# Softmax attention on one core: the row maxima turned in float16 into the sums' bank, the scores 64 times smaller, and the output product moved beside the value block

## The reference, cut to what matters

```python
q = split_heads(x @ Wq.T)
k = split_heads(x @ Wk.T)
v = split_heads(x @ Wv.T)
sim = jnp.einsum('bhid,bhjd->bhij', q, k) * DIM_HEAD ** -0.5
m = jnp.max(sim, axis=-1, keepdims=True)
e = jnp.exp(sim - m)
attn = e / (jnp.sum(e, axis=-1, keepdims=True) + 1e-10)
out = jnp.einsum('bhij,bhjd->bhid', attn, v)
return out.transpose(0, 2, 1, 3).reshape(B, N, INNER) @ Wo.T + bo
```

## Time and profile before

| what | value |
|---|---|
| median of three runs | 2273.55 us (2270.85 to 2274.36) |
| the profiled execution | 2278.47 us, its span 2276.7 us |
| busy over the span: PE / DVE / POOL / ACT | 1866.1 / 1669.5 / 1080.2 / 1066.1 us |
| reduction for the maxima, line 694 | 512 of 680 ns |
| Exp, line 795 | 512 of 597 ns |
| reciprocal, line 716 | 64 of 3353 ns |
| transposition of the maxima, line 847, in the stage | 124 recorded, median 273 ns |

### The profile page before, as it was taken

The page is one execution under the profiler, slowest core; times in us unless marked ns, Lnnn a source line. Parts: engine busy times, 40 slices in busy tenths (PEclk is TensorE's granted clock), DMA queues, the critical chain, the costliest instruction groups (busy, mean ns, idle before and its releaser), DMA issues. The chain is left out here.

```text
span 2276.7 us, 36764 instructions
## 1 busy us (share of the span) xinstructions
PE 1866.1 (82%) x12205; PEld 1097.1 (48%) x12205; DVE 1669.5 (73%) x3322; ACT 1066.1 (47%) x2294; POOL 1080.2 (47%) x1304
## 2 busy tenths in 40 slices
PE   0555489999999999999935548999948888789999
PEld 0334234444444444444414435666637677656665
DVE  5887677888788877888778875666667777746665
ACT  0112255555555555555511135555537667445555
POOL 0111255555555555555611134555545556345555
PEclk9888599999999999999968977999979999879999
DMA  6000122222222222222100000000000000000000
GB/s 181 0 0 1 28 56 63 61 59 56 60 60 61 57 57 62 60 61 57 43 0 1 0 1 1 1 0 0 0 0 1 1 1 1 1 1 9 9 9 9
DMA packets 77058, 64.53 MB, mean 28 GB/s; under 512 B 12224, under 2 KB 75904, under 8 KB 76928
## 3 DMA queue, kind: packets, MB, share of 16 engines
q1 hardware_dynamic: 71392, 57.41, 9.9%
q10 hardware_dynamic: 5536, 5.52, 0.8%
HBM read 10.32 MB, written 2.10 MB: 5 GB/s over the span
## 5 line engine op out<-in xcount | busy, mean ns | idle before, releaser
L795 ACT ACTIVATE at_pT<-at_turned 128x512 f32<-128x512 f32 x512 | 305.6, 597 | 292.2 <-PE at_turned L862 273.3
L1022 POOL TENSOR_TENSOR m_g<-m_gT,m_g 128x512 f16<-128x512 f32 x260 | 301.4, 1159 | 232.1 <-ACT m_g L1005 232.1
L1036 PE MATMUL m_h<-m_xT,m_w 128*128 (+1 forms) x1572 | 386.8, 383 | 19.9 <-PEq L463 19.9
L694 DVE TENSOR_REDUCE at_nmax<-at_score 128x1 f32<-128x512 f32 x512 | 337.2, 680 | 71.8 <-PE at_score L839 68.7
L673 POOL TENSOR_TENSOR m_w_attn<-at_pT 128x512 f32<-128x512 f32 x128 | 162.4, 1269 | 377.1 <-ACT at_pT L795 377.1
L972 DVE TENSOR_TENSOR m_gT<-m_silu,m_h 128x512 f32<-128x512 f32 x262 | 180.3, 688 | 200.5 <-ACT m_silu L1001 200.4
L1001 ACT ACTIVATE m_silu<-m_h 128x512 f32<-128x512 f32 x262 | 156.6, 598 | 227.1 <-PE m_h L1036 227.1
L716 DVE RECIPROCAL m_w_attn<-m_w_attn 128x512 f32<-128x512 f32 x64 | 214.6, 3353 | 38.6 <-ACT m_w_attn L801 38.6
L900 PE MATMUL at_pv<-at_pT,at_v 128*64 128x512 f32 x1024 | 231.4, 594 | 0.0
L1055 PEld LDWEIGHTS m_y<-m_w,m_g 128*128 128x128 f16 x3072 | 192.9, 98 | 60.5
L1036 PEld LDWEIGHTS m_h<-m_xT,m_w 128*128 128x128 f16 x1572 | 144.3, 99 | 149.6 <-issue 28.3
(11 more groups left out here) (231 smaller groups left out, 3262.6 us busy)
## 6 DMA issues: line engine op xcount, KB each, us to landing
at_both<-at_part_q SPq DMA_DIRECT2D x128, 128.0 KB, 2.4
at_kh<-at_part_k SPq DMA_DIRECT2D x256, 64.0 KB, 2.0
at_both<-at_part_q SPq DMA_DIRECT2D x128, 64.0 KB, 2.0
at_kl<-at_part_k SPq DMA_DIRECT2D x128, 64.0 KB, 2.0
m_x<-in_x SPq DMA_DIRECT2D x8, 256.0 KB, 4.7
at_both<-at_mrow SPq DMA_DIRECT2D x128, 1.0 KB
out_x<-m_x SPq DMA_DIRECT2D x8, 256.0 KB, 2.3
m_wqkv<-in_w_qkv ACTq DMA_DIRECT2D x1, 1152.0 KB, 6.6
```

Source lines behind the costliest of these rows:

```text
L694: nc.vector.tensor_reduce(nmax[head][:, qt:qt + 1], score[use % 2][:], AX.X, ALU.max, negate=True)\
L795: nc.scalar.activation(pT[g % 2][:, head, kt, :], turned[i % 2][:], ACT.Exp).then_inc(exp_done, 1)
L1022: nc.gpsimd.tensor_tensor(g16[u % 4][:, 1, :], gT[u % 4][:], g16[u % 4][:, 0, :], ALU.subtract).then_inc(low_done, 1)
L1036: last = nc.tensor.matmul(bank[:], mem["w12_16"][:, w_part, e, first:first + P], mem["xT"][:, x_part, ds(b * SEQ, SEQ)], start=(i == 0), s ...
```

## The change

The scales of both q and k are divided (by 4 and by 16), so that the scores and maxima are 64 times smaller, and Exp multiplies by 64; the weight in `kl` for the max row becomes 1. `nmax` is float16, a float16 copy of the identity is made once, and the maxima are turned by a plain matmul against it into the first 128 columns of the bank `sums` instead of a score bank, with semaphores `m_done` and `m_out` of their own. The score banks are then used by the scores alone. On DVE and SP the max row of head 0 moves: behind the reciprocal on DVE, behind all DMAs of k on SP. On TensorE the order at i = 3 becomes: projection of k, output product, value block, transposition of head 0. The core of the diff:

```diff
-        M_UNIT = 64.0
+        SHRINK = 64.0
+        SCALES = (DH ** -0.5 / W_ATTN / 4.0, 1.0 / W_ATTN / 16.0)
...
-        nmax = [s.sb(f"nmax{i}", [P, P]) for i in range(2)]
+        nmax = [s.sb(f"nmax{i}", [P, P], F16) for i in range(2)]
+        ident16 = s.sb("ident16", [P, P], F16)
...
                 def max_row(g, head):
-                    sp.wait_ge(s_read, turn_use(g, head) + 1)
+                    sp.wait_ge(m_out, 2 * g + head + 1)
...
-                    if live(g + 1):
-                        max_row(g + 1, 0)
-                    if live(g + 2):
                         sp.wait_ge(hi_done, 2 * (g + 2) + 2)
                         to_rows(g + 2, 1, 0)
                         sp.wait_ge(lo_done, 2 * (g + 2) + 2)
                         to_rows(g + 2, 1, 1)
+                    if live(g + 1):
+                        max_row(g + 1, 0)
...
                 def neg_max(g, i):
-                    dve.wait_ge(s_done, use + 1)
-                    nc.vector.tensor_reduce(nmax[head][:, qt:qt + 1], score[use % 2][:], AX.X, ALU.max, negate=True)\
+                    dve.wait_ge(s_done, UPP * g + i + 1)
+                    nc.vector.tensor_reduce(nmax[head][:, qt:qt + 1], score[i % 2][:], AX.X, ALU.max, negate=True)\
...
                 def max_row(g, head):
-                    dve.wait_ge(s_done, use + 1)
+                    dve.wait_ge(m_done, 2 * g + head + 1)
                     if g:
                         dve.wait_ge(m_in[head], 16 * g)
-                    nc.vector.tensor_scalar(mrow[head][:], score[use % 2][0:TPB, 0:P], 1.0 / M_UNIT, None, ALU.mult)\
-                      .then_inc(s_read, 1)
+                    nc.vector.tensor_copy(mrow[head][:], sums[0:TPB, 0:P]).then_inc(m_out, 1)
...
+                nc.vector.tensor_copy(ident16[:], mem["ident"][:]).then_inc(set_up, 1)
...
-                    last = nc.vector.memset(kl[i][DH:DH + 1, :, :], M_UNIT)
+                    last = nc.vector.memset(kl[i][DH:DH + 1, :, :], 1.0)
...
                         low(g + 2, 0)
-                    if live(g + 1):
-                        max_row(g + 1, 0)
-                    if live(g + 2):
                         low(g + 2, 1)
                     if live(g - 1):
                         inv_total(g - 1)
                     if live(g + 1):
+                        max_row(g + 1, 0)
                         neg_max(g + 1, 4)
                         neg_max(g + 1, 5)
...
-                    nc.scalar.activation(pT[g % 2][:, head, kt, :], turned[i % 2][:], ACT.Exp).then_inc(exp_done, 1)
+                    nc.scalar.activation(pT[g % 2][:, head, kt, :], turned[i % 2][:], ACT.Exp, scale=SHRINK)\
+                      .then_inc(exp_done, 1)
...
                 def max_turned(g, head):
-                    pe.wait_ge(s_read, score_use(g, head * TPB + TPB - 1) + 1)
-                    bank_free(use)
-                    nc.tensor.transpose(score[use % 2][:, 0:P], nmax[head][:], mem["ident"][:]).then_inc(s_done, 1)
+                    pe.wait_ge(s_read, UPP * g + (head + 1) * TPB)
+                    if 2 * g + head:
+                        pe.wait_ge(m_out, 2 * g + head)
+                    if g >= 2:
+                        pe.wait_ge(total_done, g - 1)
+                    nc.tensor.matmul(sums[:, 0:P], nmax[head][:], ident16[:], start=True, stop=True).then_inc(m_done, 1)
...
                 def values(g):
...
+                    pe.wait_ge(m_out, min(2 * g + 4, M_ALL))
...
                         if i == 3:
+                            if live(g + 2):
+                                project(g + 2, 1)
                             if live(g - 2):
                                 output(g - 2)
-                            if live(g + 2):
-                                project(g + 2, 1)
+                            if live(g - 1):
+                                values(g - 1)
                             if live(g + 1):
                                 max_turned(g + 1, 0)
-                            if live(g - 1):
-                                values(g - 1)
```

More of the change, by code:

```diff
@@ L594, in attn_stage @@
         (set_up, proj_done, hi_done, lo_done, v_out, s_done, s_read, t_done, exp_done, chain, added, sums_done, total_done,
-         rinv_done, pv_done, o_done, out_done, biased, x_added) = (s.sem(n) for n in (
+         rinv_done, pv_done, o_done, out_done, biased, x_added, m_done,
+         m_out) = (s.sem(n) for n in (
              "set_up", "proj_done", "hi_done", "lo_done", "v_out", "s_done", "s_read", "t_done", "exp_done", "chain",
-             "added", "sums_done", "total_done", "rinv_done", "pv_done", "o_done", "out_done", "biased", "x_added"))
+             "added", "sums_done", "total_done", "rinv_done", "pv_done", "o_done", "out_done", "biased", "x_added", "m_done",
+             "m_out"))
         s_in = [s.sem(f"s_in{i}") for i in range(RING)]
@@ L604, in attn_stage @@
         PERIODS = range(-2, PAIRS_ALL + 2)
[L606 to L617, removed]
+        M_ALL = 2 * PAIRS_ALL
         with nc.Block() as block:
@@ L691, in neg_max @@
                     head, qt = divmod(i, TPB)
-                    use = score_use(g, i)
-                    dve.wait_ge(s_done, use + 1)
-                    nc.vector.tensor_reduce(nmax[head][:, qt:qt + 1], score[use % 2][:], AX.X, ALU.max, negate=True)\
+                    dve.wait_ge(s_done, UPP * g + i + 1)
+                    nc.vector.tensor_reduce(nmax[head][:, qt:qt + 1], score[i % 2][:], AX.X, ALU.max, negate=True)\
                       .then_inc(s_read, 1)
                 def max_row(g, head):
-                    use = turn_use(g, head)
-                    dve.wait_ge(s_done, use + 1)
+                    dve.wait_ge(m_done, 2 * g + head + 1)
                     if g:
                         dve.wait_ge(m_in[head], 16 * g)
-                    nc.vector.tensor_scalar(mrow[head][:], score[use % 2][0:TPB, 0:P], 1.0 / M_UNIT, None, ALU.mult)\
-                      .then_inc(s_read, 1)
+                    nc.vector.tensor_copy(mrow[head][:], sums[0:TPB, 0:P]).then_inc(m_out, 1)
                 def low(g, which):
                     dve.wait_ge(hi_done, 2 * g + 1 + which)
-                    scale = (DH ** -0.5 / W_ATTN, 1.0 / W_ATTN)[which]
+                    scale = SCALES[which]
                     pair = part[which]
@@ L733, in _ @@
                 nc.vector.memset(nmax[0][:], 0.0)
-                nc.vector.memset(nmax[1][:], 0.0).then_inc(set_up, 1)
+                nc.vector.memset(nmax[1][:], 0.0)
+                nc.vector.tensor_copy(ident16[:], mem["ident"][:]).then_inc(set_up, 1)
                 for i in range(RING):
@@ L826, in _ @@
                 XY = [(0, 0), (0, 1), (1, 0)]
-                def bank_free(use):
-                    if use >= 2:
-                        pe.wait_ge(s_read, use - 1)
                 def scores(g, i):
                     head, qt = divmod(i, TPB)
-                    use = score_use(g, i)
+                    use = UPP * g + i
                     k = g % RING
@@ L837, in scores @@
                         pe.wait_ge(s_in[k], 16 * S_DMAS * (g // RING + 1))
-                    bank_free(use)
-                    nc.tensor.matmul(score[use % 2][:], both[k][:, 0, head, qt * P:(qt + 1) * P], kh[k][:, head, :], start=True,
+                    if use >= 2:
+                        pe.wait_ge(s_read, use - 1)
+                    nc.tensor.matmul(score[i % 2][:], both[k][:, 0, head, qt * P:(qt + 1) * P], kh[k][:, head, :], start=True,
                                      stop=True).then_inc(s_done, 1)
                 def max_turned(g, head):
-                    use = turn_use(g, head)
-                    pe.wait_ge(s_read, score_use(g, head * TPB + TPB - 1) + 1)
-                    bank_free(use)
-                    nc.tensor.transpose(score[use % 2][:, 0:P], nmax[head][:], mem["ident"][:]).then_inc(s_done, 1)
+                    pe.wait_ge(s_read, UPP * g + (head + 1) * TPB)
[4 more added lines that the diff above has]
+                    nc.tensor.matmul(sums[:, 0:P], nmax[head][:], ident16[:], start=True, stop=True).then_inc(m_done, 1)
                 def scores_turned(g, i):
```

## The result

| | before | changed |
|---|---|---|
| median of four runs | 2272.38 us (2270.85 to 2274.36) | 2301.12 us (2298.92 to 2302.22) |
| ratio, 95% interval | 1 | 1.0124 [1.0108, 1.0140] |
| span of the profiled execution | 2276.7 us | 2298.7 us |
| first to last start of the reciprocal, 63 periods | 844.8 us | 871.1 us |

A forecast was written before the change was run, and what follows sets the result against it. The prediction took TensorE to set the pace in the attention stage; its terms gave +0.46 us per period, +28.5 over 62 periods, and with small terms +28 together, so 2301.5 us, with 2284 to 2330 for 8 in 10.

The forecast's parts named there:

- The order at i = 3: TensorE, attention stage: output product moved behind k's projection leaves an idle gap before the projection, +1.11 us per period.
- The hidden wait of 0.21: TensorE: k's projection waits 0.21 us for q's low part behind the output product; no longer separate, -0.21 per period.
- Fewer turns in the score banks: TensorE: score 2 waits for the older maximum of score 0 instead of score 1's; gain 0.31 us per period.
- the float16 turn: TensorE: each of two transpositions shrinks from 0.20 to 0.056 us as a float16 matmul; gain 0.29 us per period.
- Score 6: TensorE waits at this matmul for maximum 4, delayed by head 0's max row behind DVE's reciprocal; cost 0.16 us per period.
- The sum: Attention stage: -0.31 -0.29 -0.21 +1.11 +0.16 = +0.46 us per period, over 62 periods +28.5 us.
- The small terms: Stage edges: batch boundaries -1 us, last two periods -1, first max row issued behind k's transfers up to +2.
- Late max row: Rival: head 0's row lands 3.6 us after issue, TensorE waits 0.8 us each period, total 2351; chance 0.14.
- Gap filled by TensorE itself: Rival: TensorE takes the output product ahead of the waiting k projection, period falls 0.44 us, total 2246; chance 0.05.
- Lower clock: Rival: idle stretches lower TensorE's granted clock in the attention stage; at 0.97, total 2325 us; chance 0.05.
- Nothing much: Rival: q's low part comes 0.3 us earlier, gap only matches the 0.81 us saved; within 5 us of 2274; chance 0.08.

The follow-up runs named there:

- float32 run: The changed kernel with nmax in float32 and the maxima turned by the float32 transposition into the sums bank; ratio 1.0123 to the kernel before.
- float16 alone: The kernel before with float16 maxima at full size, turned by a plain float16 matmul into the score banks in the old order; ratio 0.9982.
- row-later run: The changed kernel with DVE's max row of head 0 behind maxima 4 and 5 instead of ahead; ratio 1.0152 to the kernel before.
- last kernel: The changed kernel with output before k's projection, q's low part before maximum 3, and head 0's max row between maxima 4 and 5; ratio 0.9827.

## Why the prediction was right

Forecast 2301.5, measured 2301.12, of which the change is +28 forecast and +28.7 measured, with an interval of 25 to 32. The mechanism is the forecast's, but such closeness is luck: two terms were off by about 0.1 us per period and cancelled, the count of 62 periods was two too high, and the medians of one and the same kernel differ by more than a microsecond (2273.55 from three runs of the kernel before, 2272.38 from four).

- *The order at i = 3, the step that carries the result:* 1.11 us was forecast before k's projection and 1.11 is what the trace shows (615.45 to 616.56). Undoing it alone turns the kernel from 1.2% slower to 1.4% faster, making it alone costs 2.2%, and starting the low part 0.19 earlier shortens the gap by 0.18. This step is shown from three sides. The output product was moved in 60 periods, not in the 62 of the sum.
- *The hidden wait of 0.21:* right. Output and k's projection came from 1.12 to 0.93 apart when the low part was made earlier.
- *Fewer turns in the score banks and the float16 turn:* for head 1 I had 0.31 + 0.144, and 0.51 fell to 0.05, so the sum was right (0.46). The split was not: float32 takes 0.10 in a full queue, and the wait was 0.41. For head 0 I had 0.144, and 0.20 fell to 0.06. But the 0.20 was read in front of the sums, and 0.09 of it is a cost of what stands in front of the sums, not of the turn. It came back behind the output product (0.98 instead of the 0.90 of the earlier trace rows). This is the mis-sized term: "2 x (0.20 - 0.056) = 0.29" is 0.20 when the 0.09 is taken off, and of that the type of the turns is only about 0.05 each. The float32 run and float16 alone show the small worth: 0.06 and 0.05 us a period.
- *Score 6:* forecast 0.16, measured 0.08. The 0.09 in front of the sums moved score 4 (T+7.91 for the forecast 7.83) and the reciprocal (T+5.16 for 5.08) alike, but maximum 4 started 0.14 behind the row instead of 0.2 and so at T+8.57, as forecast (8.56). TensorE had less left to wait; score 6 is at T+9.29 in both.
- *The sum:* -0.31 - 0.29 - 0.21 + 1.11 + 0.16 = +0.46 by the forecast, 13.92 - 13.46 = +0.46 in the trace. Its parts there are -0.46 for head 1, -0.14 for head 0, -0.21, +1.11, +0.09 and +0.08, which is 0.47 with the rounding.
- *The small terms:* at the seven batch boundaries the period went from 13.95 to 14.29, so the change costs 0.12 less there than elsewhere, -0.8 for the forecast -1. The last periods were to gain 0.6 each; one gained 0.42 (11.92 to 11.50) and the other lost 0.07 (10.71 to 10.78). The up to +2 at the start can't be told from the 41.2 to 43.8 us by which ten traces vary there.
- *Late max row:* did not happen, and the row-later run prices it: landing 1.76 us, margin 1.06. The fixed cost of some 2 us that the prediction takes from the Trainium skill (DMA: Bandwidth & Descriptors, Anatomy of one DMA) is fitted there for transfers issued by GpSimd; this row goes out through SP and came in a little sooner.
- *Gap filled by TensorE itself:* the trace has the output product behind the projection in every period seen, with TensorE idle ahead of it. *Lower clock:* 1.00 in the stage, as before. *Nothing much:* the low part of q follows score 3 by 1.02, not earlier. The sign named for this rival, a low part "that follows score 3 by less than 1.5 us", can't be read by the start, for that was 1.03 before the change already; read by the end of the low part it holds against the rival, 1.71 before and 1.70 after.

What stays open is what the 0.09 in front of the sums is. The sums and values are 64-column products into halves of a bank, all others are full width; the profile has the first weight load of the sums beginning when their first matmul does (both at 618.20 in the changed kernel), while that of a float16 turn lies 0.21 ahead of it (607.60 and 607.81 in float16 alone). No run changed that by itself. Likewise open is why the float32 turn takes 0.16 us behind the value block and 0.10 elsewhere.

## What to carry to other kernels

When the busiest engine's instructions are reordered, look for what each one covers: here the output product stood in the 1.11 us in which another engine made the operand of the next instruction, and moving it cost its whole length, more than the two real gains of the change brought. Read the cost of an instruction in a stream of its kind, not from the distance to a different kind of neighbour, and expect nothing from shortening one that stands ahead of a wait. To price a transfer without a landing time, delay its issue until someone waits for it.

## What was not expected of the hardware

- A float32 turn of 128 columns by transposition takes 0.10 us in a full queue, twice the 0.05 of the float16 matmul of the same size. Behind the value block it takes 0.16, the float16 one 0.06.
- In front of the 64-column float32 sums stands about 0.09 us that the instruction ahead does not explain: behind a float16 projection (0.75 for 0.65), the float32 output product (0.98 for 0.89) and a float16 turn (0.15 for 0.06) alike.
- The 1 KB row from four partitions into one landed 1.76 us after the start of its issue, against a median of 2.0 for 64 KB; in two periods of the last kernel it took 2.45 and 2.65. The Trainium skill, DMA: Bandwidth & Descriptors, Specifications, says that pieces under 512 B are read, modified and written. The row's four pieces are of 256 B (128 float16 each); no extra time for that shows in these runs, and none has the same row in larger pieces.
- Behind the same idle stretch of 2.60 us the float32 sums at the stage's end ran at a granted clock of 0.86 to 0.89 over that step in six traces (four records in 1.9 to 2.0 us) and at 0.98 to 1.00 in four (1.08 us). No run shows what decides.
